# Norms by token on centred weights in a fused two-layer attention kernel, with two loads and a key rotation moved

## The reference

```python
def _L0_xattn_ref(decoder_hidden, encoder_output, Wqkv, Wout, b_out, Wgate, b_gate, gamma, beta):
    # 16 heads of 8; rotary queries and keys; scores + a bias over positions; softmax; values
    attended = attended @ Wout.T + b_out
    gate = jax.nn.sigmoid(attended @ Wgate.T + b_gate)
    return gate * attended + (1.0 - gate) * residual
def _L0_ffn_ref(x, weight, aux_weight1, aux_weight2, bias):
    h = x @ weight @ aux_weight1 @ aux_weight2
    return jnp.tanh(h + bias)
x = x + _L0_xattn_ref(_layernorm(x), ctx_1024, ...)
x = x + _L0_ffn_ref(_layernorm(x), ...)
x = x + _L1_xattn_ref(_layernorm(x), ctx_1024, ctx_1024, mask, wq, bq, ...)   # queries: y = x @ wq.T + bq
x = x + _L1_ffn_ref(_layernorm(x), ...)                                       # 8 experts, best 2
```

## Time and profile before

| | us |
|---|---|
| timed runs, median of 3 | 582.25 |
| lowest, highest | 575.12, 584.12 |
| profiled execution | 577.29 |
| its span | 575.9 |
| TensorE busy | 514.1 |
| ScalarE busy | 431.5 |
| VectorE busy | 276.9 |
| POOL busy | 171.5 |

### The profile page before, as it was taken

The page is one execution under the profiler, slowest core; times in us unless marked ns, Lnnn a source line. Parts: engine busy times, 40 slices in busy tenths (PEclk is TensorE's granted clock), DMA queues, the critical chain, the costliest instruction groups (busy, mean ns, idle before and its releaser), DMA issues.

```text
span 575.9 us, 15324 instructions
## 1 busy us (share of the span) xinstructions
PE 514.1 (89%) x6330; PEld 257.7 (45%) x6330; DVE 276.9 (48%) x715; ACT 431.5 (75%) x493; POOL 171.5 (30%) x207
## 2 busy tenths in 40 slices
PE   7688898997979998899999999999999999999993
PEld 4344445444435554455455444434443444344341
DVE  4838555864585255752521342235263435254145
ACT  1257576786678786787879988898979888988841
POOL 4467727584586316750010001000001000000003
PEclk9889999999999999999999999999999999999996
DMA  8497965399258513582364474129213911100000
GB/s 287 102 311 200 290 210 144 117 276 309 64 172 262 194 43 89 176 259 62 81 126 136 116 159 110 31 74 204 78 40 89 218 48 39 32 1 2 10 1 16
DMA packets 51584, 74.53 MB, mean 129 GB/s; under 512 B 11146, under 2 KB 40050, under 8 KB 51506
## 3 DMA queue, kind: packets, MB, share of 16 engines
q1 hardware_dynamic: 40690, 37.92, 26.4%
q0 software_dynamic: 5632, 24.07, 12.3%
q10 hardware_dynamic: 5184, 11.48, 6.3%
HBM read 39.95 MB, written 18.83 MB: 102 GB/s over the span
## 4 chain that ended last, share of the span: by engine, by line
PE 54%; ACT 16%; issue 9%; DVE 9%; POOL 6%; DMA 4%; SPq 1%; ACTq 0%; DVEq 0%; POOLq 0%
PE ps L505 21%; ACT probs L1132 14%; PE ps L481 14%; DMA q_side<-in_far_q 4%; PE ps L416 3%; PE ps L406 2%; PE ps L591 2%; DVE k_swapped L1430 2%; PE ps L410 1%; PE ps L517 1%; ACT k_parts L1159 1%; PE ps L665 1%; PE ps L541 1%; POOL k L977 1%; POOL k L979 1%
## 5 line engine op out<-in xcount | busy, mean ns | idle before, releaser
L1132 ACT ACTIVATE probs<-ps 124x1024 f32<-124x1024 f32 (+1 forms) x416 | 398.6, 1024 | 78.5 <-PE ps L486 51.2
L505 PE MATMUL ps<-probs,values 124*9 124x256 f32 (+1 forms) x3328 | 218.6, 380 | 0.1
L481 PE MATMUL ps<-q_side,k_side 64*124 64x256 bf16 (+1 forms) x1664 | 163.2, 290 | 37.2 <-ACT probs L1132 29.9
L481 PEld LDWEIGHTS ps<-q_side,k_side 64*124 64x124 bf16 (+1 forms) x1664 | 79.3, 130 | 139.9 <-ACT probs L1132 99.9
L505 PEld LDWEIGHTS ps<-probs,values 124*9 124x9 f32 (+1 forms) x3328 | 70.7, 90 | 87.0 <-issue 27.8
L1003 POOL TENSOR_TENSOR post_rstd<-post_rstd,power 128x2 f32<-128x2 f32 x12 | 8.4, 702 | 153.5 <-DVE post_rstd L1627 93.7
L949 POOL DMA_DIRECT2D mask_q<-in_mask x16 | 9.1, 570 | 131.2 <-DVE checks L1489 112.1
L486 PE MATMUL ps<-bias_near,bias_w 64*124 64x84 bf16 (+1 forms) x416 | 42.6, 200 | 0.0
L1430 DVE SCALAR_TENSOR_TENSOR k_swapped<-ps,beta_products,k_table_sb 32x496 f32<-32x496 f32 (+2 forms) x64 | 40.4, 632 | 0.9
L1499 DVE TENSOR_REDUCE sample_max<-ps 128x8 f32<-128x512 f32 x32 | 20.5, 685 | 34.9 <-PE ps L439 34.9
L416 PE MATMUL ps<-w_centred,ctx_turned 128*124 128x256 f32 (+1 forms) x104 | 31.2, 424 | 3.0 <-DVE k_swapped L1430 1.3
(11 more groups left out here) (234 smaller groups left out, 517.7 us busy)
## 6 DMA issues: line engine op xcount, KB each, us to landing
k_side<-k_scratch SPq DMA_DIRECT2D x24, 400.2 KB, 8.6
k_side<-k_parts SPq DMA_DIRECT2D x48, 124.0 KB, 2.4
k_scratch<-k_parts POOLq DMA_DIRECT2D x16, 372.0 KB, 5.2
q_side<-q_parts SPq DMA_DIRECT2D x63, 64.0 KB, 2.4
v_scratch<-values POOLq DMA_DIRECT2D x4, 936.0 KB, 10.7
values<-v_scratch SPq DMA_DIRECT2D x4, 936.0 KB, 13.8
v_scratch<-v POOLq DMA_DIRECT2D x12, 288.0 KB, 5.5
mask_q<-in_mask POOLq DMA_DIRECT2D x8, 400.5 KB, 3.4
```

Source lines behind the costliest of these rows:

```text
L481: last = pe.matmul(ps[0:width, bank, SQ * i:SQ * (i + 1)], kst[rows, j % 2, 2 * g + i, at], qst[rows, query_slot(j, run), 2 * g + i, :], s ...
L505: last = pe.matmul(ps[32 * i:32 * i + VC, ACC + g // 2, SQ * (g % 2):SQ * (g % 2) + SQ], v[0:rows, j % 2, t, h, :], p[0:rows, u % 4, SQ * ...
L1132: act.activation(p[0:rows, u % 4, :], ps[0:rows, s:s + 2, :].rearrange("p a n -> p (a n)"), ACT.Exp)\
```

## The change

Both norms of the gate are taken by token: two products with the identity turn the batch's columns into token rows in PSUM (`post_tokens`), VectorE takes `bn_stats` and `bn_aggr` of these, and the weight product runs on the un-normed columns with weights whose input side was centred once (a third step of `fold_weights`). VectorE multiplies the product by the spread factor; the tanh then reads SBUF. The gate has five steps, in slots 38, 40, 43, 45, 48 (8, 10, 13, 15, 18 in passes 3 and 4), and the fold steps start one slot earlier. On ScalarE's queue the token rows of batch 3 are loaded after unit 15 of pass 1 instead of 8; on POOL's, the first mask piece after the first chunk's parts and stores of batch 2 instead of before them. In pass 2 VectorE rotates chunk 2 of batch 3's keys between the high and the middle part of the queries. `row_deviations` stands only where it did. Cut (names of semaphores are left out):

```diff
@@ -125,7 +125,7 @@
 CENTRE_X_AT = ((0, 20), (0, 34))
-FOLD_AT = ((1, 8), (1, 9))
+FOLD_AT = ((1, 7), (1, 8), (1, 9))
 PICK_AT = 3
@@ -142,9 +142,8 @@
         return None
-    base = 38 if j < NB - 1 else 8
-    steps = (0, 2, 3, 5, 6, 8, 9, 11, 12)
-    return steps.index(slot - base) if slot - base in steps else None
+    steps = (38, 40, 43, 45, 48) if j < NB - 1 else (8, 10, 13, 15, 18)
+    return steps.index(slot) if slot in steps else None
@@ -193,7 +192,9 @@
         post = sb("post", [128, 4 * SQ])
-        po, pg, psq, ph = (post[:, SQ * i:SQ * (i + 1)] for i in range(4))
+        po, pg, post_stats, ph = (post[:, SQ * i:SQ * (i + 1)] for i in range(4))
+        pst = post_stats[:, 0:12].rearrange("p (t s) -> p t s", s=6)
+        pmv = post_stats[:, 12:16].rearrange("p (t s) -> p t s", s=2)
         prs = sb("post_rstd", [128, 2])
...
@@ -529,23 +530,30 @@
                       .then_inc(made[LOW], 1)
-                else:
+                elif k == 1:
                     pe.wait_ge(folds, 1)
...
                     pe.matmul(ps[:, HIGH, 128:256], late["ffn_wt"][:], w_a12[:], start=True, stop=True).then_inc(made[HIGH], 1)
-            def post_mean(bank, what, b):
-                fill(bank, *what)
-                pe.matmul(ps[:, bank, 0:SQ], ones_mean[:], x[:, columns(b)], start=True, stop=True).then_inc(made[bank], 1)
-            def post_var(bank, what, k):
-                pe.wait_ge(sq_ready, k + 1)
-                fill(bank, *what)
+                else:
+                    pe.wait_ge(seen[HIGH], side.of(HIGH, "fold"))
+                    fill(LOW, "centred")
+                    pe.matmul(ps[:, LOW, 0:128], centre[:], w_123[:], start=True, stop=True)
+                    pe.matmul(ps[:, LOW, 128:256], centre[:], late["L1_wq"][:], start=True, stop=True).then_inc(made[LOW], 1)
+            def post_tokens(b, k, weights_in, what):
+                pe.wait_ge(resid, 2 * b + 1 + k)
+                fill(LOW, "tokens", 2 * b + k)
                 for t in range(TT):
-                    last = pe.matmul(ps[:, bank, t:t + 1], psq[:, 128 * t:128 * t + 128], ones_mean[:, 0:1], start=True, stop=True)
-                last.then_inc(made[bank], 1)
+                    last = pe.matmul(ps[:, LOW, 128 * t:128 * t + 128], x[:, b * SQ + 128 * t:b * SQ + 128 * t + 128], ident[:],
+                                     start=True, stop=True)
+                last.then_inc(made[LOW], 1)
+                pe.wait_ge(folds, 3)
+                fill(HIGH, what, b)
+                pe.matmul(ps[:, HIGH, 0:SQ], weights_in, x[:, columns(b)], start=True, stop=True).then_inc(made[HIGH], 1)
@@ -563,18 +571,12 @@
                     pe.matmul(ps[:, HIGH, 0:SQ], w_og[:], att[:, columns(b)], start=True, stop=True).then_inc(made[HIGH], 1)
-                elif k in (1, 5):
-                    pe.wait_ge(resid, 2 * b + 1 + (k == 5))
-                    post_mean(LOW, ("mean", 2 * b + (k == 5)), b)
-                elif k in (2, 6):
-                    post_var(HIGH, ("var", 2 * b + (k == 6)), 2 * b + (k == 6))
-                elif k in (3, 7):
-                    post_spread(LOW, ("spread", 2 * b + (k == 7)), 2 * b + (k == 7))
+                elif k == 1:
+                    post_tokens(b, 0, w_123[:], "ffn")
+                elif k == 3:
+                    post_tokens(b, 1, late["L1_wq"][:], "q1")
                 else:
-                    pe.wait_ge(seen[LOW], side.of(LOW, "spread", 2 * b + (k == 8)))
-                    fill(HIGH, "ffn" if k == 4 else "q1", b)
-                    pe.matmul(ps[:, HIGH, 0:SQ], w_123[:] if k == 4 else late["L1_wq"][:], xn[:, columns(b)], start=True, stop=True)\
-                      .then_inc(made[HIGH], 1)
+                    post_spread(LOW, ("spread", 2 * b + (k == 4)), 2 * b + (k == 4))
@@ -997,7 +999,7 @@
                 if k < 2 * NB:
-                    pool.wait_ge(seen[HIGH], side.of(HIGH, "var", k))
+                    pool.wait_ge(post_var, k + 1)
                 else:
@@ -1087,11 +1089,11 @@
                     norm_context(b, n)
-                if b == 2:
-                    look_at_mask(0)
                 for n in range(NC):
                     store_keys(b, n)
+                    if b == 2 and n == 0:
+                        look_at_mask(0)
                     if b == 1 and n == 2:
@@ -1136,11 +1138,9 @@
                     act.activation(pg[:], ps[:, HIGH, 0:SQ], ACT.Tanh, bias=half_bz[:, 0:1], scale=0.5).then_inc(seen[HIGH], 1)
-                elif k == 4:
-                    if b:
-                        act.wait_ge(q1_lo, b)
-                    act.wait_ge(made[HIGH], side.of(HIGH, "ffn", b))
-                    act.activation(ph[:], ps[:, HIGH, 0:SQ], ACT.Tanh, bias=col["b_ffn"]).then_inc(seen[HIGH], 1)
+                elif k == 2:
+                    act.wait_ge(post_normed, 2 * b + 1)
+                    act.activation(ph[:], ph[:], ACT.Tanh, bias=col["b_ffn"]).then_inc(ffn_done, 1)
@@ -1228,7 +1228,7 @@
                     load_turned(2 if i == 2 else 3)
-                elif (j, i) == (1, 8):
+                elif (j, i) == (1, 15):
                     load_token_rows(3)
@@ -1273,7 +1273,7 @@
                     middle_queries(1)
-                if gate_at(j, i - 3) in (0, 4):
+                if gate_at(j, i - 3) in (0, 2):
                     gate(j - 1, gate_at(j, i - 3))
@@ -1476,6 +1476,9 @@
                 rotate_keys(b, n)
+                rest_of_keys(b, n)
+            def rest_of_keys(b, n):
                 both_values(b, n, 0)
@@ -1549,28 +1552,41 @@
                     dve.tensor_copy(w_a12[:], ps[:, LOW, 256:384]).then_inc(seen[LOW], 1)
-                else:
+                elif k == 1:
                     dve.wait_ge(made[HIGH], side.of(HIGH, "fold"))
...
                     dve.tensor_copy(w_123[:], ps[:, HIGH, 128:256]).then_inc(seen[HIGH], 1)
-            def centre_post(bank, k, b):
-                cols = columns(b)
-                dve.wait_ge(made[bank], side.of(bank, "mean", k))
-                dve.tensor_tensor(xn[:, cols], x[:, cols], ps[:, bank, 0:SQ], ALU.subtract).then_inc(seen[bank], 1)
-                dve.wait_ge(seen[bank], side.of(bank, "mean", k))
-                dve.tensor_tensor(psq[:], xn[:, cols], xn[:, cols], ALU.mult).then_inc(sq_ready, 1)
-            def deviate_post(bank, k):
-                dve.wait_ge(made[bank], side.of(bank, "var", k))
-                dve.tensor_scalar(prs[:], ps[:, bank, 0:TT], EPS, None, ALU.add).then_inc(seen[bank], 1)
-            def norm_post(bank, k, b):
-                cols = columns(b)
-                dve.wait_ge(made[bank], side.of(bank, "spread", k))
-                dve.tensor_tensor(xn[:, cols], xn[:, cols], ps[:, bank, 0:SQ], ALU.mult).then_inc(seen[bank], 1)
+                else:
+                    dve.wait_ge(made[LOW], side.of(LOW, "centred"))
+                    dve.tensor_copy(w_123[:], ps[:, LOW, 0:128])
+                    dve.tensor_copy(late["L1_wq"][:], ps[:, LOW, 128:256]).then_inc(seen[LOW], 1)
+                    dve.wait_ge(seen[LOW], side.of(LOW, "centred"))
+                    dve.sem_inc(folds, 1)
+            def post_norm(b, k, what):
+                n = 2 * b + k
+                dve.wait_ge(made[LOW], side.of(LOW, "tokens", n))
+                for t in range(TT):
+                    last = dve.bn_stats(pst[:, t, :], ps[:, LOW, 128 * t:128 * t + 128])
+                last.then_inc(seen[LOW], 1)
+                dve.wait_ge(seen[LOW], side.of(LOW, "tokens", n))
+                for t in range(TT):
+                    last = dve.bn_aggr(pmv[:, t, :], pst[:, t, :])
+                last.then_inc(post_aggr, 1)
+                dve.wait_ge(post_aggr, n + 1)
+                dve.tensor_scalar(prs[:], pmv[:, :, 1], EPS, None, ALU.add).then_inc(post_var, 1)
+                dve.wait_ge(made[HIGH], side.of(HIGH, what, b))
+                dve.tensor_copy(pg[:], ps[:, HIGH, 0:SQ]).then_inc(seen[HIGH], 1)
+                if k == 0 and b:
+                    dve.wait_ge(q1_lo, b)
+                dve.wait_ge(seen[HIGH], side.of(HIGH, what, b))
+                dve.wait_ge(made[LOW], side.of(LOW, "spread", n))
+                dve.tensor_tensor(ph[:], pg[:], ps[:, LOW, 0:SQ], ALU.mult).then_inc(seen[LOW], 1)
+                dve.wait_ge(seen[LOW], side.of(LOW, "spread", n))
+                dve.sem_inc(post_normed, 1)
@@ -1585,27 +1601,29 @@
                    .then_inc(resid, 1)
-                centre_post(LOW, 2 * b, b)
-                deviate_post(HIGH, 2 * b)
-                norm_post(LOW, 2 * b, b)
-                dve.wait_ge(seen[HIGH], side.of(HIGH, "ffn", b))
+                post_norm(b, 0, "ffn")
+                dve.wait_ge(ffn_done, b + 1)
                 dve.tensor_tensor(x[:, cols], x[:, cols], ph[:], ALU.add).then_inc(resid, 1)
-                centre_post(LOW, 2 * b + 1, b)
-                deviate_post(HIGH, 2 * b + 1)
-                norm_post(LOW, 2 * b + 1, b)
+                post_norm(b, 1, "q1")
```

(23 more changed lines are left out.)

8 lines of the change are left out of this document (4 added, 4 removed).

## The result

| | before | after |
|---|---|---|
| timed runs, median of 20 | 580.66 us | 577.21 us |
| lowest, highest | 575.12, 585.00 | 571.36, 580.84 |
| ratio of the times | | 0.994, 95% interval 0.9911 to 0.997 |
| profiled execution, its span | 577.29, 575.9 | 577.65, 576.2 |

The account below looks back on a forecast made before the run. Late passes were held bound by ScalarE's exponentials, those carrying keys and gates by TensorE's list and its stops. Terms summed to −5.15 us, giving 577.1 from the 582.25 median; forecast a little lower, 576, range 568 to 585.

Parts of the forecast that it names:

- the hole: Pass 1: TensorE's 2.66 us stall for the third run's far query rows, plus slow products after it, closes; −4.3 us.
- fold step: Two new 128-column products on centred weights in TensorE's list, and a short wait for VectorE's copy; +0.75 us, once.
- mask piece on POOL: Batch 2's keys: issuing the mask load now sits in POOL's busy chain, which VectorE and TensorE wait for; +0.7 us.
- gates: Five steps for nine: less TensorE work per norm, a longer wait for the tanh; −0.3 us each, −1.1 for four.
- pass 1's far rows: Pass 1: the last run's scores stood 0.40 us for far rows; the longer wait ahead covers that; −0.4 us.
- rotation: Pass 2: key rotation fills VectorE's gap between query parts, so TensorE no longer waits for the rotated keys; −0.8 us.
- The walk through one gate: Pass 3, followed slot by slot: TensorE's second tokens wait 0.8 us on VectorE's sum; −0.3 us per gate.
- The rival of the tanh: Gates: the wait for the tanh grows; at 2 us more per gate the kernel is slower, 585.1 us; 1 in 8.
- that of the token rows: Batch 3's token rows land after 154.4 us and delay VectorE, each us late costing the pass one; under 1 in 20.
- the hole stays: Pass 1: far rows still land at 142.9, the fold hides in the stall, slow clock stays; 580.6 us; 2 in 10.
- more than I count: Slower timed runs owe their 7 us to longer holes of this kind, and all go; about 570 us; about 1 in 16.

Follow-up runs that it names:

- e11: The changed kernel with only the mask piece put back ahead of batch 2's parts; first to last sums product 422.66 us, for 423.26 in the changed kernel.
- e2: The changed kernel with both loads and the rotation put back, leaving gate and fold step; first to last sums product 424.56 us, for 428.35 before.

## Why the prediction was right

Term by term, by periods of TensorE's list in the changed kernel against the kernel before:

| step | forecast | measured |
|---|---|---|
| the hole | −4.3 | −4.37 (4.15 for 8.52) |
| fold step | +0.75 | +0.86 |
| mask piece on POOL | +0.7 | +0.6 (+0.63 by e11) |
| gates | −1.1 | −1.5 (−0.39, −0.39, −0.39, −0.31) |
| pass 1's far rows | −0.4 | −0.1 (its gate −0.47, less the −0.39 of pass 2's) |
| rotation | −0.8 | −0.85 (pass 2 of e2: 71.69, of after: 70.84) |
| sum, first to last sums product | −5.15 | −5.1 and −4.9 (two pairs of traces) |

The steps' periods add up to −5.3; the 0.2 to the passes' −5.1 is lost later in passes 3 and 4, which end 0.34 and 0.19 us shorter for their gates' 0.39 and 0.31. The walk through one gate held best: the second tokens wait 0.72 to 0.73 us where 0.8 stood, and each gate gains 0.3 to 0.4. The rival of the tanh fell, since that wait doesn't vary between the four gates; so did that of the token rows, which landed at 150.0 and were first read at 160.3, and that of the hole that stays.

Four things in the text were weaker than its total.

*Two terms that erred against one another.* The far rows' 0.40 us at the end of pass 1 were priced as a cost of their own; they stood in place of the gate's usual 0.30 us and gave 0.1. The gates gave 0.4 more than their −1.1. That the sum is right to 0.1 us is luck to this extent.

*The reason for the hole's end.* It says that 1.23 MB less backlog let the far rows land 3.3 us sooner, with 1.4 us of margin. The rows did come in time, but the bytes are not the measure: one load of the two is enough, and with none moved the fold step alone cuts the hole from 8.52 to 5.05. The rival "the hole stays" had it that the fold's 0.75 would hide in the stall and the slow clock stay: e2 is the nearest case, with no load moved, and there the slow clock did not stay. In the kernel as changed the two loads together are worth 0.3 us in pass 1 (75.54 in e2, 75.24 after), hardly more than the 0.25 by which its three traces differ, and the token rows without the mask piece 0.9 (74.61 in e11). The terms were added as if independent; the hole was shared by three of them.

*The spread.* I expected waits such as the hole to be what varies, and put "more than I count" at 570. But the hole's wait was 2.66 to 3.01 us in three traces. The larger source was pass 0's wait in front of unit 4, 1.6 to 2.2 us in some traces and 7.5 to 9.8 in others. The changed kernel's own runs still reach from 571 to 581. The row was in the trace before, 1.89 us at 37.03, and I had not asked what it would be in an execution whose first stretch runs at full clock.

*From the sum to the median.* 582.25 was a median of three; with twenty runs it is 580.66, and 5.15 less is 575.5 for the measured 577.2. The intervals of both chips (1.7 to 5.2 us and 1.3 to 5.4 us) hold the 5.1 us of the traces at their upper edge. Whether the total gives less than the passes do, as the medians suggest, isn't settled: a change that leaves pass 0 alone should leave the share of its long waits alone too, and the runs are too few to tell.

## What to carry to other kernels

When two profiled executions are equally long, compare them between marks inside the program before saying that nothing changed: here a gain of 5.1 us and an unrelated loss of 5.8 cancelled. When several edits bear on one stall, ask which of them would close it alone, test them alone, and keep the cheapest (here the token rows without the mask piece). When two waits follow one another, ask whether the first only stands in place of the second before pricing both. And look at what a program issues in its first 40 us on each DMA queue: bulk loads that VectorE first reads 20 to 24 us later (49.74 and 55.51 in the changed kernel's trace), issued ahead of a piece that the next unit waits for, cost more in that execution than all four gates gain.

## What the runs showed of the hardware

A wait of 2.66 to 3.01 us in TensorE's list was followed by a granted clock of 0.61 to 0.67, part of the stretch at 1.2 GHz; a wait of 0.83 us at the same place left it at 1.00. From 28 to 32 us the granted clock was 0.57 to 0.70 in some executions and 1.00 in others of one and the same kernel; why is open. The two executions of the changed kernel with 1.00 there ended 4.6 and 5.6 us later than the one with 0.61: a 124 KB key piece issued behind 768 KB of bulk loads of another queue landed after 11.6 us, and after 4.0 us where these loads came behind it. VectorE's cast of 128x496 took 1.32 us beside a POOL subtraction and 0.42 alone.
